# A 1-core Trainium2 kernel: expert rows scaled on ScalarE and summed in PSUM, routing as a stage of its own, positions chosen anew

## The reference

```python
xn = layernorm(x)
x  = x + latent_attention(xn) + moe(xn)      # 16 heads of 8, causal
def moe(x):                                   # 8 experts, the best 2 for each token
    logits = x @ Wg + bg
    gates  = softmax(where(in_top_2, logits, -inf))
    for e in range(8):
        out += gates[..., e:e+1] * (relu(x @ W1[e] + b1[e]) @ W2[e] + b2[e])
```

## Time and profile before

| | us |
|---|---|
| median of 3 runs | 1763.05 (1761.45 to 1764.23) |
| the profiled execution | 1766.17 |
| its span, first to last instruction | 1764.4 |
| PE / DVE / ACT / POOL busy | 1512.7 / 1218.0 / 1036.8 / 810.6 |
| mean granted TensorE clock, share of 2.4 GHz | 0.938 |

### The profile page before, as it was taken

How to read it: one execution, slowest core, us unless ns; L and a number is a source line. 1 busy time by engine, 2 the same in 40 slices (tenths; PEclk the granted TensorE clock), 3 DMA queues, 4 the chain that set the end, 5 groups by cost and what they waited for, 6 DMA issues and landing times.

```text
span 1764.4 us, 33697 instructions
## 1 busy us (share of the span) xinstructions
PE 1512.7 (86%) x11337; PEld 648.1 (37%) x11337; DVE 1218.0 (69%) x3199; ACT 1036.8 (59%) x2258; POOL 810.6 (46%) x728
## 2 busy tenths in 40 slices
PE   2685898899989998999889998999899988889876
PEld 1352452245323543335323543345333543332221
DVE  5554578667876688767885788767886778577532
ACT  2372474667547765677647765677557765736532
POOL 5156346435644447354644556345645453513142
PEclk9997798999889999999999999999999999979975
DMA  6751551136211542126211542136212531101010
GB/s 226 246 156 59 145 156 41 42 109 175 67 46 49 140 126 79 34 85 185 75 46 48 156 120 70 41 96 180 64 44 73 154 103 25 50 23 37 1 37 7
DMA packets 138876, 159.35 MB, mean 90 GB/s; under 512 B 15744, under 2 KB 100304, under 8 KB 137808
## 3 DMA queue, kind: packets, MB, share of 16 engines
q1 hardware_dynamic: 134608, 148.79, 29.0%
q0 software_dynamic: 4096, 8.40, 1.6%
HBM read 115.96 MB, written 40.85 MB: 89 GB/s over the span
## 4 chain that ended last, share of the span: by engine, by line
PE 55%; DVE 18%; issue 9%; ACT 6%; POOL 5%; DMA 3%; SPq 3%; another core or an unknown queue 1%; POOLq 0%; DVEq 0%; ACTq 0%
PE banks L438 53%; DVE negmax L838 8%; ACT probs L1187 2%; ACT hm L1256 2%; POOL h_lo L1441 1%; DMA qkc<-relm 1%; DVE h L1071 1%; DVE xs L1006 1%; POOL xslots L1375 1%; PE banks L694 1%; DVE h L1066 1%; SPq L1532 1%; DMA xslots<-kp 1%; DVE r_b L1096 1%; DVE g_t L1061 1%
## 5 line engine op out<-in xcount | busy, mean ns | idle before, releaser
L1187 ACT ACTIVATE probs<-banks 128x512 f32<-128x512 f32 (+3 forms) x1216 | 581.4, 534 | 384.5 <-PE banks L438 358.1
L838 DVE TENSOR_REDUCE negmax<-banks 128x1 f16<-128x512 f32 x768 | 493.0, 685 | 147.3 <-PE banks L438 139.9
L834 DVE CUSTOM_DVE_ANT_0 scr<-banks,mask_row 128x384 bf16<-128x384 f32 (+3 forms) x512 | 230.1, 486 | 172.2 <-PE banks L438 170.5
L438 PE MATMUL banks<-kp,qs 32*128 32x512 f16 (+3 forms) x1024 | 242.4, 361 | 64.1 <-DMA kp<-relk 26.7
L438 PE MATMUL banks<-probs,vp 128*32 128x512 f32 (+3 forms) x2048 | 242.6, 548 | 1.4 <-POOL probs L1353 1.4
L438 PE MATMUL banks<-qs,kp 32*128 32x512 f16 (+3 forms) x1024 | 216.8, 351 | 22.5 <-ACT probs L1187 15.9
L1381 POOL TENSOR_TENSOR hl<-hm,hh 128x512 f16<-128x512 f32 x120 | 139.2, 1160 | 149.9 <-DVE hh L1001 149.9
L1401 POOL TENSOR_TENSOR psums<-psums,probs 128x1024 f32<-128x1024 f32 x64 | 149.2, 2355 | 111.9 <-PE banks L438 110.7
L1441 POOL TENSOR_TENSOR h_lo<-h,h_hi 128x512 f16<-128x512 f32 x96 | 112.2, 1189 | 162.5 <-DVE h_hi L1079 101.6
L1256 ACT ACTIVATE hm<-banks,wt 128x128 f32<-128x128 f32 x480 | 137.9, 375 | 82.6 <-PE banks L438 81.7
L438 PE MATMUL banks<-qkc 97*128 97x512 f16 (+1 forms) x512 | 170.6, 406 | 12.9 <-DMA qkc<-pack 3.9
(11 more groups left out here) (209 smaller groups left out, 2412.3 us busy)
## 6 DMA issues: line engine op xcount, KB each, us to landing
wt<-wexp SPq DMA_DIRECT2D x120, 258.0 KB, 3.0
wt<-wexp SPq DMA_DIRECT2D x120, 256.0 KB, 3.0
qkc<-relm SPq DMA_DIRECT2D x96, 128.0 KB, 3.2
qs<-relq SPq DMA_DIRECT2D x64, 128.0 KB, 2.7
kp<-relk SPq DMA_DIRECT2D x64, 128.0 KB, 2.9
relm<-halves SPq DMA_DIRECT2D x32, 256.0 KB, 2.1
xg<-xslots SPq DMA_DIRECT2D x24, 256.0 KB, 3.0
yslots<-yv SPq DMA_DIRECT2D x24, 256.0 KB, 3.6
```

The source lines that it names most:

```text
L438: return nc.tensor.matmul(psum[rows_, bank, cols_], lhsT, rhs, start=start, stop=stop)
L834: v.tensor_tensor_reduce(scr[:, s, 0:kw], psum[:, SCO + s, 0:kw], mask_row[:, T - kw:T], -1.0, 3e38, ALU.add, ALU.min, negmax[:, g.n % 2, ...
L838: v.tensor_reduce(negmax[:, g.n % 2, NC * h + c:NC * h + c + 1], psum[:, SCO + s, 0:kw], AX.X, ALU.max, negate=True).then_inc(sem("max"), 1)
L1187: a.activation(keys(g, c)[:, 2 * pair + s, q0:T], psum[:, TRA + s, q0:T], ACT.Exp, scale=SCALE[main(g)]).then_inc(sem("exp"), 1)
```

## The change

1. The DVE addition (L1002 to L1012) is removed, with its semaphore x_moe. ACT scales the gathered rows in place instead, 8 activations of 128x128 at places 52 (k = 0) and 51 (k = 1), after all gathers have landed and gk is there. PE adds both halves into bank M with two fp32 matmuls against the identity, each over 512 columns, behind the four products with l0_o; it waits for both scalings first. The gathers of the next batch wait for that PE group (m_full) instead of x_moe. `pick` waits for the scalings of the batch before and tells ACT through a semaphore gk.
2. The routing (rank, gex, gates, pos, starts, slots, addresses, pick, scatter, first two xg_load) is a stage "route" with a MOVE of its own: 6 steps later in batch 0. Scatters go from places -27..-24 to -16, -15, -16, -15, the two table loads from -22, -21 to -5, -4, pick from -24 to -10, slots from -27 to -25.
3. `keep_warm` issues 4 unread matmuls (128x512, fp16) at each of 10 steps in batch 0 (warm0) and 10 in batch 7 (warm1), after waiting for a maximum that is long there in those steps.
4. Some 30 other positions move by one or two steps, among them lat and its norm, xT1_out, q1_out, ca_o, mck, up, down, two weight loads, and wo1 with store (one step earlier).

The diff, without the table lines in which nothing named above moves:

```diff
-MOVE = {"front": {}, "prep": {0: 11}, "ca": {-1: -24}, "mid": {-1: -24}, "last": {-1: -30},
-        "ffn": {-1: -24}, "tail": {-2: -12, -1: -52}}
+MOVE = {"route": {0: 6}, "warm0": {-1: -6}, "warm1": {-1: 6}, "front": {}, "prep": {0: 11},
+        "ca": {-1: -24}, "mid": {-1: -24}, "last": {-1: -30}, "ffn": {-1: -24}, "tail": {-2: -12, -1: -52}}
...
-      "xr_lo": -42, "lat": -37, "lat_stat": -37, "lat_root": -35, "lat_norm": -34, "latT": -33, "latT_out": -32, "q0": -34,
+      "xr_lo": -42, "lat": -36, "lat_stat": -36, "lat_root": -34, "lat_norm": -33, "latT": -33, "latT_out": -32, "q0": -34,
-      "pos": -29, "starts": -27, "slots": -27, "addresses": -25, "pick": -24, "add": 55, "v0a": 3, "v0a_out": 4, "v0b": 30,
+      "pos": -29, "starts": -27, "slots": -25, "addresses": -25, "pick": -10, "v0a": 3, "v0a_out": 4, "v0b": 30,
-      "x1_root": 65, "x1_norm": 66, "xT1": 67, "xT1_out": 68, "xl1": 72, "cg": 71, "cg_out": 71, "mod": 72, "q1": 73,
-      "q1_out": 74, "q1_low": 75, "q1_send": 76, "k1": 75, "k1_out": 76, "k1_low": 75, "k1_send": 78, "caq": 77,
+      "x1_root": 65, "x1_norm": 66, "xT1": 67, "xT1_out": 69, "xl1": 72, "cg": 71, "cg_out": 71, "mod": 72, "q1": 73,
+      "q1_out": 75, "q1_low": 75, "q1_send": 76, "k1": 75, "k1_out": 76, "k1_low": 75, "k1_send": 78, "caq": 77,
-AT.update({("up", i): at for i, at in enumerate((10, 12, 13, 16, 17, 20, 22, 24, 25, 29, 30, 32, 34, 36, 38), 0)})
-AT.update({("down", i): at for i, at in enumerate((13, 15, 17, 19, 21, 23, 25, 27, 29, 31, 33, 35, 37, 39, 42), 0)})
+AT.update({("up", i): at for i, at in enumerate((9, 12, 13, 16, 17, 20, 22, 24, 25, 29, 30, 32, 34, 35, 38), 0)})
+AT.update({("down", i): at for i, at in enumerate((13, 15, 17, 19, 21, 23, 25, 27, 31, 32, 33, 35, 37, 39, 42), 0)})
-AT.update({("scatter", i): at for i, at in enumerate((-27, -26, -25, -24), 0)})
+AT.update({("scatter", i): at for i, at in enumerate((-16, -15, -16, -15), 0)})
-AT.update({("xg_load", i): at for i, at in enumerate((-22, -21, 7, 19), 0)})
+AT.update({("xg_load", i): at for i, at in enumerate((-5, -4, 7, 19), 0)})
-AT.update({("w_store", i): at for i, at in enumerate((-11, -10, -1, 2), 0)})
+AT.update({("w_store", i): at for i, at in enumerate((-11, -10, -4, 2), 0)})
-AT.update({("load", i): at for i, at in enumerate((1, 14, 24), 4)})
+AT.update({("warm0", i): at for i, at in enumerate((34, 37, 43, 47, 48, 51, 58, 65, 66, 70), 0)})
+AT.update({("warm1", i): at for i, at in enumerate((178, 181, 186, 188, 192, 192, 194, 194, 197, 199), 0)})
+AT.update({("scale", i): at for i, at in enumerate((52, 51), 0)})
+AT.update({("load", i): at for i, at in enumerate((1, 14, 25), 4)})
...
+    elif head in ("warm0", "warm1"):
+        STAGE[name_] = head
+    elif head.startswith("rank") or head in ("gex", "gates", "pos", "starts", "slots", "addresses", "pick", "scatter") \
+            or name_ in (("xg_load", 0), ("xg_load", 1)):
+        STAGE[name_] = "route"
...
-DUE = {(time(name, b), name): b for name in AT for b in range(B)}
+def batches(name):
+    return (0,) if name[0] == "warm0" else (B - 1,) if name[0] == "warm1" else range(B)
+
+
+DUE = {(time(name, b), name): b for name in AT for b in batches(name)}
...
+                def keep_warm(G):
+                    for k in range(10):
+                        if due(G, ("warm0", k)) is not None or due(G, ("warm1", k)) is not None:
+                            g, j = UNIT[max(at for at in UNIT if at <= G)]
+                            pe.wait_ge(sem("max"), 2 * (8 * g.n + j) + 1)
+                            for _ in range(4):
+                                mm(SCO, slice(0, T), ident16[:, :], ident16[:, :].unsqueeze(1).broadcast_to([P, NC, P]), True, True)
...
                     if (b := due(G, "wo0")) is not None:
                         taken(pe, "m", "back0", b)
                         for c in range(NC):
-                            last = mm(M, ch(c), oT[:, ch(c)], W("l0_o"), False, c == NC - 1)
+                            mm(M, ch(c), oT[:, ch(c)], W("l0_o"), False, False)
+                        pe.wait_ge(sem("scaled"), 2 * b + 2)
+                        for k in range(2):
+                            last = mm(M, slice(0, T), C("ident"), yg[:, NC * k:NC * k + NC, :].rearrange("p c d -> p (c d)"), False, k == 1)
                         last.then_inc(sem("m_full"), 1)
...
                     turn_over(G)
+                    keep_warm(G)
...
-                    link(v.tensor_reduce(gk[:, :, :], first[:, :, :, :], AX.X, ALU.add))
+                    if b:
+                        dve.wait_ge(sem("scaled"), 2 * b)
+                    v.tensor_reduce(gk[:, :, :], first[:, :, :, :], AX.X, ALU.add).then_inc(sem("gk"), 1)
+                    dve.wait_ge(sem("gk"), b + 1)
...
-                    if (b := due(G, "add")) is not None:
-                        dve.wait_ge(sem("gath"), 128 * (b + 1))
-                        for k in range(2):
-                            for c in range(NC):
-                                ins = v.scalar_tensor_tensor(out=xs[:, b % 4, c, :], in0=yg[:, NC * k + c, :],
-                                                             scalar=gk[:, k, c:c + 1], in1=xs[:, b % 4, c, :],
-                                                             op0=ALU.mult, op1=ALU.add)
-                            if k == 0:
-                                link(ins)
-                        ins.then_inc(sem("x_moe"), 1)
-                        dve.wait_ge(sem("x_moe"), b + 1)
...
+                    for k in range(2):
+                        if (b := due(G, ("scale", k))) is not None:
+                            act.wait_ge(sem("gath"), 128 * (b + 1))
+                            act.wait_ge(sem("gk"), b + 1)
+                            for c in range(NC):
+                                ins = a.activation(yg[:, NC * k + c, :], yg[:, NC * k + c, :], ACT.Copy, scale=gk[:, k, c:c + 1])
+                            ins.then_inc(sem("scaled"), 1)
...
-                                    pool.wait_ge(sem("x_moe"), b)
+                                    full(pool, "m", "wo0", b - 1)
```

More of the change, by code:

```diff
@@ L116 @@
 AT = {"l1_split": 14, "x_load": -59, "x_stat": -50, "x_root": -49, "x_norm": -48, "xT0": -39, "xT0_out": -38, "xr_hi": -43,
-      "xr_lo": -42, "lat": -37, "lat_stat": -37, "lat_root": -35, "lat_norm": -34, "latT": -33, "latT_out": -32, "q0": -34,
+      "xr_lo": -42, "lat": -36, "lat_stat": -36, "lat_root": -34, "lat_norm": -33, "latT": -33, "latT_out": -32, "q0": -34,
       "q0_out": -33, "q0r": -32, "q0r_out": -31, "q0_sum": -30, "q0_send": -27, "k0": -19, "k0_out": -18, "k0r": -16,
       "k0r_out": -15, "k0_sum": -15, "k0_send": -12, "rank0": -35, "rank1": -32, "rank2": -33, "gex": -33, "gates": -29,
-      "pos": -29, "starts": -27, "slots": -27, "addresses": -25, "pick": -24, "add": 55, "v0a": 3, "v0a_out": 4, "v0b": 30,
+      "pos": -29, "starts": -27, "slots": -25, "addresses": -25, "pick": -10, "v0a": 3, "v0a_out": 4, "v0b": 30,
       "v0b_out": 29, "gT": 39, "gT_out": 40, "back0": 53, "back0_out": 54, "wo0": 57, "wo0_out": 58, "x1_stat": 63,
[2 rows of a table removed]
[2 rows of a table added]
       "caq_out": 78, "caq_low": 79, "caq_send": 80, "cak": 79, "cak_out": 79, "cak_low": 82, "cak_send": 82,
       "ca_spread": 109, "cav": 112, "cav_out": 113, "v1": 129, "v1_out": 130, "bo": 100, "ca_div": 136, "ca_mul": 141,
-      "ca_o": 142, "ca_o_out": 144, "gelu1": 151, "gelu2": 166, "f3": 171, "f3_out": 173, "f3_add": 172, "back1": 181,
-      "ctx": 181, "mcq": 205, "mcq_out": 205, "mcq_low": 207, "mcq_send": 209, "mck": 207, "mck_out": 208, "mck_low": 209,
-      "mck_send": 212, "mc_spread": 217, "mcv": 220, "mcv_out": 221, "mc_div": 249, "mc_mul": 250, "mc_o": 254,
-      "mc_o_out": 255, "ctx2": 256, "wo1": 257, "wo1_out": 257, "store": 258}
+      "ca_o": 143, "ca_o_out": 145, "gelu1": 151, "gelu2": 166, "f3": 171, "f3_out": 173, "f3_add": 172, "back1": 181,
+      "ctx": 181, "mcq": 205, "mcq_out": 205, "mcq_low": 207, "mcq_send": 209, "mck": 208, "mck_out": 209, "mck_low": 210,
+      "mck_send": 213, "mc_spread": 217, "mcv": 220, "mcv_out": 221, "mc_div": 249, "mc_mul": 250, "mc_o": 254,
+      "mc_o_out": 255, "ctx2": 256, "wo1": 256, "wo1_out": 256, "store": 257}
 AT.update({("spread0", i): at for i, at in enumerate((-7, -5, 5, 17), 0)})
@@ L146 @@
 AT.update({("y_store", i): at for i, at in enumerate((20, 29, 37, 43), 0)})
-AT.update({("w_store", i): at for i, at in enumerate((-11, -10, -1, 2), 0)})
+AT.update({("w_store", i): at for i, at in enumerate((-11, -10, -4, 2), 0)})
 AT.update({("turn", i): at for i, at in enumerate((72, 6, 47), 0)})
-AT.update({("split", i): at for i, at in enumerate((-12, -11, -2, 3, 9, 21, 35), 0)})
-AT.update({("load", i): at for i, at in enumerate((1, 14, 24), 4)})
+AT.update({("warm0", i): at for i, at in enumerate((34, 37, 43, 47, 48, 51, 58, 65, 66, 70), 0)})
```

(10 more changed lines are left out.)

2 lines of the change are left out of this document (1 added, 1 removed).

## The result

The changed kernel takes 1746.55 us (1742.88 to 1751.61), the kernel before 1763.06 in the same runs: ratio 0.9902, 95% interval 0.9883 to 0.9921, 16.5 us faster. The forecast was 1737 in a range of 1716 to 1757, so 26 us faster: right in sign and in the range, with 0.63 of the gain.

What follows compares the result with a forecast made beforehand. PE was taken to bound the average, DVE places 53 to 60, and no engine the start, transition and end. Terms -8 + 1.5 - 2 - 3 - 10.5 + 0 - 0.5 - 3.5 = -26 gave 1737 us, range 1716 to 1757.

Steps and rivals of the forecast that it cites:

- The start: Batch 0's key path: k0_sum, ahead of the scatters, starts about 29, ten us earlier; -8 us, bounds -10 and -5.
- the thirty small moves: Other positions shifted by a place or two, slack behind each: 0, between -0.5 and +0.5 us a batch.
- Bursts before the transition: Three bursts in batch 0's expert chain cost PE time, the other seven are covered by idle time: +1.5 us.
- The transition: Batch 0 to 1: additions gone, but scatters still ahead of k0_sum in POOL's queue; k0_sum moves by -2 us.
- products at half clock late: Transition's upper bound: k0_sum +2 us, since k0 and k0r follow wo0 on PE, which waits for ACT's scalings.
- The clock: First scores of batch 1: bursts raise PE's clock only partly, given the gap's idle tail; -3 us of (-10, 0).
- The DVE-bound stretch: Places 53 to 60, batches 1 to 7: DVE loses 3.2 us, PE gains two products; -1.5 each, -10.5 in all.
- ACT's scaling: Places 51 and 52: eight activations, 2.3 us, fit in ACT's slack before the exponentials; 0.
- Scatters and small moves: Scatters at 64 and 65 delay k0_sum by about 4 us, hidden in batches 1 to 7; with other moves, -0.5.
- The end: Last 32.9 us at clock 0.60: bursts raise the clock; -3.5 us, at most -6.5, or +2.5 if it doesn't rise.
- everything delivers: Rival: clock held through both gaps and the DVE stretch gives its full 3.2; -48, 1715 us; chance 0.12.
- The rival of the slower kernel: Products at the lower clock level cost 3.9; with ACT's 2.3, places 51 to 58 grow 3.0 a batch; 1775 us; chance 0.07.

Runs made afterwards that it cites:

- part one alone: The kernel before with only item 1 of the change (ACT scales, PE adds), every position as before: 1738.73 us, ratio 0.9919.
- the chip of the second: The changed kernel timed again, unedited, on another chip: 1746.24 us, ratio 0.9968, with the kernel before at 1752.17.

## Why the prediction was right or wrong

**The start, forecast -8: wrong.** -0.7 to place 0, and +2.3 by place 31. The step that failed is "so it starts about 29": the input, there at 28.92 before, is there at 33.94. The working moved the routing on POOL and on SP and forgot that it is on DVE too, where its ranks and weights now stand in front of k0's products. Then the first two of k0_sum's three instructions took 3.9 longer beside DVE's conversions. The copy, for which contention was feared, took 4.47 instead of 4.69. Not moving the routing costs only 2.7 at place 0 and nothing in the total.

**Another loss there, not in the sum:** places 7 to 11 of batch 0 by 3.5, by the split that was moved along with up 0. It was among "the thirty small moves", costed at 0.

**Bursts before the transition, forecast +1.5: not seen.** Without any burst the transition was 66.4 against 66.2.

**The transition, forecast -2: wrong, +3.8.** That the scatters "are still ahead of k0_sum" and set its start failed: the last is over at 173.3, 3.0 before k0_sum's input comes, and k0r behind wo0, the identity products and ACT's scalings took their place ("products at half clock late", the bound of +2). In part one alone this new chain is exactly as long as the scatters it replaces: k0_sum at 170.28 against 170.09. What makes it longer in the changed kernel are the positions of lat, down and up: put back, 3.4 return; which of the three does it wasn't separated.

**The clock, forecast -3: not delivered.** From batch 1's first maxima on, 27.4 us were granted 0.57 in the kernel before, 0.57 in the changed kernel and 0.57 without bursts. What the bursts raised is the gap ahead of that (0.74 from 151 to 185 us, against 0.60 without), where it bought nothing that can be seen. 80 to 160 did fall by 3.5 in the first pair of traces, but by 0.5 in the second (180.7 to 180.2), and takes 180.5 without bursts. The prediction's reason for taking only 3 of 10 was the idle tail of the gap, and that tail took the rest too: behind the last burst the clock was granted in full (1.00 from 182 to 184 us) while PE was busy 0.51 of the 2.00 us, and from 186 us on, with the scores begun, it was at its lower level (0.50 up to 195).

**The DVE-bound stretch, forecast -1.5 each: the size about right, in part by luck.** At the same clock the additions' 2.3 came back as 2.2 at place 55, and the products cost 1.3 at place 57, near the 1.7 taken. The pick's 0.9 hardly came back: places 53 to 57 fell by 2.3 with it and by 2.2 without. That is 0.9 a batch for part one, not 1.5. The term that the sum left out is the clock, which in the kernel before falls at place 57 in three or four of six batches and with the products on PE doesn't: 1.1 where it fell. On the first chip the same stretch gave more still, since in the kernel before it held late results and, at place 60, a low clock; with the moved scatters both are mostly gone. The moved scatters weren't separated from the rest on such a chip.

**ACT's scaling, 0: right.** Eight in 2.5 us before the exponential, which waits 0.61 for PE in the changed kernel; the Trainium skill's advice against ScalarE for such work (ScalarE: Activation LUTs, Rules for kernel authors) didn't bear here, where each took 0.32. Only in the transition, where the gather ends last, do its 2.5 us lie on the path.

**Scatters and small moves, forecast -0.5: wrong twice, in opposite ways.** The moved scatters gave 1.0 a batch, at place 66; q1_out, inside "0, between -0.5 and +0.5 a batch", cost 1.4 a batch, some 10 in all, of the terms for the middle the largest error. The bound was set without following what is queued behind k1 on PE.

**The end, forecast -3.5: -2.3** by the last stage, and the bursts are what give it (37.9 without).

**The sum:** -26 was forecast, -16.5 measured in the first comparison and -5.9 on the chip of the second. With q1_out and the transition's positions back it is 30, of the 48 that "everything delivers" had. That the number fell into the range is luck in good part. By the table the start, the transition and the bursts came to +6.1 where -8.5 was forecast, and all from step 80 to 739 to -18.3 where -14 was forecast. And 11 of the 16.5 us are there only because the kernel before takes 11 longer on the first chip; at the ratio of the second (0.9968) the forecast's 1763 would have become 1757.4, just outside the range. The rival of the slower kernel failed at its first step: it took the lower level for the products of place 57 from one batch, and in batches 1 to 7 of the changed kernel the pair ran at the higher one, in 1.88.

## What to carry to other kernels

When a step moves past others, list what it passes on each engine that it uses, the vector engine too, and for each result that is read out of a shared bank ask which product needs that bank next and what is queued behind it: one place later for one copy-out cost 1.4 us in each batch, more than half of what the whole restructuring gave. Before a shorter stretch is put down to the work that was moved, compare batches with the same granted clock: here half of the 2.0 us was a fall of the clock that no longer came. Change positions one group at a time and measure stages by fixed points in the order of work rather than by totals; here two good parts (some 1.7 a batch by the medians, and 1.0) were half hidden by one bad line. And a change to a kernel whose time differs by chip has to be compared on the same chip.

## What the runs showed of the hardware

**DVE and POOL wait for each other by whole instructions.** POOL's sum of k0 took 3.24 beside DVE's long conversions, 1.27 without them, and its rounding 2.55 instead of 0.61; the second of the conversions took 3.35 instead of 2.28:

```profile
33.85 2.28 DVE L1178 TENSOR_TENSOR wt<-probs,wt 128x2048 f16<-128x2048 f32 x1
34.01 3.24 POOL L1442 TENSOR_TENSOR w<-r_a,r_b 128x512 f32<-128x512 f32 x1 [10.07 <-DVE r_b L889]
36.05 3.35 DVE L1178 TENSOR_TENSOR yg<-probs,hm 128x2048 f16<-128x2048 f32 x1
37.31 2.55 POOL L1444 CAST halves<-w 128x512 f16<-128x512 f32 x1
```

The conversion that started first took its usual 2.28; the sum ended 1.12 behind it, the next conversion 2.15 behind the sum, the rounding 0.46 behind that. In the run with the additions back, the first of them (2.30) ended 0.15 behind POOL's sums and the second (1.24) 0.15 behind POOL's next instruction; the other six took 0.34 or 0.35 as ever, and POOL's sums lost nothing (2.33 each, 2.36 on the page's mean). The Trainium skill (SBUF — State Buffer, SBUF: two separate sides) says that the two engines share a pair of ports under a lock that whoever starts first holds for a whole instruction, for a DVE operation with two SBUF inputs when POOL's reads SBUF. The rows agree: both kinds of DVE instruction have two such inputs, and each time it is the later one that waits. A position chosen anew can bring such a pair together.

**The kernel before differs by chip, the changed one didn't.** It took 1751 to 1771 on five chips, the changed kernel 1746.6 and 1746.2 on two, where the kernel before had 1763.1 and 1752.2. What the traces show of it is the late results at the end of eight scatters, some 1 us each in five batches, and the clock behind them. Two other kernels had their scatters at the old places and show none, on the chips of 1752 us. On the chip of 1771 us, two kernels with moved scatters show one each (1.57 and 1.52), at the end of eight gathers. Why some chips show it isn't settled; no run here separates it from other causes.
